# One subtraction of an attention kernel issued on GpSimd instead of VectorE

## The chip, the cores and the metric

The kernel runs on all 8 cores of one Trainium2 chip, the same program on each, with no traffic between cores. Core c takes batch c // 2 and one half of its 4096 positions as queries (2048 of them, "own"), with all 4096 positions as keys. The time is device time of the slowest core in microseconds.

## What is computed

X is (4, 4096, 1024), 16 heads of width 64, EPS = 1e-4:

```
xn = layernorm(x)
Q, K, V, G = split(xn @ W_in + b_in)              # per head, 64 columns each
W = (EPS + sqrt(max(|q|^2 + |k|^2 - 2 q.k, 0))) ** -2
A = (W / (EPS + sum_s W)) @ V
x = x + concat_heads(G * A) @ W_out + b_out
x = x + layernorm(x) @ sign(weight).T
```

The kernel doesn't take the square root. With D the squared distance, (EPS + sqrt(D))^-2 is about 1/D - 2 EPS D^-1.5, and both powers come from one logarithm: L = Ln(D), Ea = Exp(-L), Ebc = Exp(-1.5 L + ln(2 EPS)), W = Ea - Ebc. The last of these, `wb`, is the subtraction that the change touches.

## The kernel before

The program is written as five queues, one for each engine, with semaphores between them. `st(engine, fn, waits, inc)` appends one instruction to an engine's queue; each engine takes its queue strictly in order and stops at the first wait that is not met. So the order in which the Python code calls `st` is the order of each queue.

Before attention, the input is normalised and transposed into XnT, and head 0 is projected. After attention come the output projection, the second layernorm and the product with the signs. None of this touches the changed line. In between, attention runs over 16 heads, 4 query blocks of 512 to a head, and 16 rounds r to a block, each for 256 keys. Two rounds make a step s of 4 x 512 = 2048 score columns; there are 32 steps to a head, 8 to a query block. What a step does:

- `emit_S` (L480, TensorE): scores of a round, two matmuls into pS. Kaug and Qaug have 66 rows, with the squared norms as two of them, so pS is the squared distance. pS has two buffers, one to a round.
- `emit_c1` (L489, ScalarE): Lb = Ln(pS), once a round.
- `emit_c24` (L495, L498, ScalarE): Ea and Ebc from Lb, once a step. Ea has two buffers and waits for the subtraction two steps back; Ebc has one, and waits for the subtraction one step back.
- `emit_c3` (L503, VectorE before): wb = Ea - Ebc, 128x2048, out in bf16, two buffers. It waits for Ebc and for the matmuls that read the wb of two steps back.
- `emit_A` (L517, TensorE): four matmuls for a step, Vs by wb, summed over the block's 8 steps in pA (row 64 sums W, since column 64 of Vs is 1).

At the end of a query block `emit_epilogue_a` copies pA to A_sb on VectorE (L531), moves its row 64 to partition 0 by a DMA issued on GpSimd (L537), takes Ln and Exp of it on ScalarE (L541, L543) and splits the result in two bf16 rows (L546, L548). `emit_epilogue_b` spreads them over partitions by matmul, multiplies, and for odd heads moves Htmp into H by another GpSimd DMA (L593).

The projections of the next head are spliced into the rounds of this one. `stage_proj` writes them down in 61 groups, the first one empty: 4 for Q, 8 for K, 32 for V, 4 for G, then 8 for the k norms and 4 for the q norms. `splice` appends about one group per round. The weights' loads on SyncE and their casts to bf16 on VectorE (L318) go in as one piece in round 0 of a head (`flush_w`). A Q, K, V or G group is eight matmuls (L333, L364) into pp and one copy out on VectorE. A norm group is a square on VectorE (KQsq, L390), one matmul (L398), a copy to the single buffer k2row on VectorE (L402) and a DMA issued on GpSimd (L407, L412) that puts it in row 64 or 65 of the next head's Qaug or Kaug. The copy waits until the DMA before it has landed. The scores of a new head wait, by a nop on GpSimd (L418), for all of these DMAs.

The main loop for round r, shortened:

```python
        emit_c1(r)
        if r % 2 == 1:
            emit_c24(r // 2)
            emit_c3(r // 2)
        if r + 1 < NTOT and not nxt_head_start:
            emit_S(r + 1)
        if r % 2 == 0 and r >= 2:
...
            emit_A(2 * s - 2)
            emit_A(2 * s - 1)
...
        splice(slot_in_head + 1, NQC * NREG)
```

Of the kernel before, what the change touches and what calls it, by code (L numbers as in the profile page):

```python
# [34 lines left out]
def build_nc():  # L35
# [11 lines left out]
    def st(engine, fn, waits=(), inc=None, inc_n=1):  # L47
        if inc is not None:
            inc.n += inc_n
        cur_steps[0][engine].append((list(waits), fn, inc, inc_n))  # L50
# [449 lines left out]
           waits=[(s_c3, s)], inc=s_c2)  # L500

    def emit_c3(s):
        st("vector", lambda e, s=s: e.tensor_tensor(  # L503
            out=wb[s % 2][:], in0=Ea[s % 2][:], in1=Ebc[:], op=ALU.subtract),
           waits=[(s_c2, 2 * s + 2), (s_wcons, max(0, 4 * s - 4))], inc=s_c3)

# [94 lines left out]
    for r in range(NTOT):  # L601
# [7 lines left out]
# [3 lines that stand above are left out]
# [3 lines left out]
        if r % 2 == 0 and r >= 2:  # L615
# [3 lines left out]
            s = r // 2  # L619
# [302 lines left out]
```

How the kernel before makes its waits and increments, by code:

```python
            def run(eng):  # L861
                for waits, fn, inc, inc_n in steps[name]:
                    for (sm, val) in waits:
                        if val > 0:
                            eng.wait_ge(sm.h, val)
                    inst = fn(eng)
                    if inc is not None:
                        inst.then_inc(inc.h, inc_n)
```

## Time and profile before

| | |
|---|---|
| median of 3 runs | 4886.65 us (4886.46 to 4899.19) |
| the profiled execution | 4886.19 us, span of its slowest core 4884.6 us |
| spans of the 8 cores | 4874.3 to 4884.6 us |
| mean granted TensorE clock | 0.668 to 0.676 of full |
| from the first Ebc to the last (attention) | 345.9 to 4533.5 us of the span |

The profile is of one execution, on the slowest core (core 5). Engines are named PE (TensorE matmul), PEld (its weight loads), DVE (VectorE), ACT (ScalarE), POOL (GpSimd) and SP (SyncE); L503 is line 503 of the kernel. In a timeline a row gives the start, the length, the engine, the line and the operation; in brackets stands how long the engine had been idle before it and what ended that. A row of POOL's DMA is the issue, not the transfer.

### The profile page before, as it was taken

How to read it: one execution, taken by the hardware profiler on the slowest of the kernel's cores; microseconds unless marked ns; L12 is line 12 of the kernel's file. 1: busy time of each engine (PE TensorE's matmuls, PEld its weight loads, DVE VectorE, ACT ScalarE, POOL GpSimd, SP SyncE). 2: the span in 40 equal slices, each digit the busy share in tenths (PEclk: the TensorE clock that was granted, in tenths of full speed). 3: DMA queues.
4: the chain of work that ended last, by engine and by line, in shares of the span. 5: the costliest groups of instructions: out<-in, count | busy, mean ns of one | idle time of the engine just before them, and what ended most of it. 6: DMA issues, size and time to landing. Idle time of an engine off the chain costs nothing.

```text
span 4884.6 us, 45463 instructions; the slowest of 8 cores (4874.3 to 4884.6 us)
## 1 busy us (share of the span) xinstructions
PE 2654.0 (54%) x11472; PEld 1049.1 (21%) x11472; DVE 2167.3 (44%) x2630; ACT 3027.2 (62%) x2321; POOL 146.3 (3%) x300
## 2 busy tenths in 40 slices
PE   1156465665655554656555565556465555645535
PEld 1122122222212121212222121212122222211202
DVE  4534444444444444444444444444444444443344
ACT  2218676676768585867767585858676776768100
POOL 0000000000000000000000000000000000000000
PEclk9977575667666675767576666666576766655757
DMA  2200000000000000000000000000000000000312
GB/s 75 66 18 1 5 6 2 10 1 10 2 10 1 9 2 10 1 1 10 2 10 1 9 2 10 1 9 2 6 5 1 10 2 8 1 1 2 104 35 69
DMA packets 41383, 64.14 MB, mean 13 GB/s; under 512 B 12992, under 2 KB 29376, under 8 KB 40128
## 3 DMA queue, kind: packets, MB, share of 16 engines
q1 hardware_dynamic: 31680, 58.79, 3.8%
q0 software_dynamic: 9472, 2.45, 0.3%
q8 instruction: 123, 2.02, 0.2%
q14 instruction: 108, 0.88, 0.1%
HBM read 50.39 MB, written 8.39 MB: 12 GB/s over the span
## 4 chain that ended last, share of the span: by engine, by line
PE 27%; ACT 25%; issue 23%; DVE 18%; DMA 6%; DVEq 1%; ACTq 0%; SPq 0%; POOLq 0%
ACT Ebc L498 13%; DVE wb L503 10%; ACT Lb L489 8%; PE pA L517 7%; PE pS L480 7%; PE pp L333 7%; DMA Wst<-w_in 2%; DMA rsrow<-A_sb 2%; PE pp L364 1%; ACT Ea L495 1%; PE pp L398 1%; PE pS L836 1%; PE pS L682 1%; DVE KQsq L390 1%; DVE A_sb L531 1%
## 5 line engine op out<-in xcount | busy, mean ns | idle before, releaser
L503 DVE TENSOR_TENSOR wb<-Ea,Ebc 128x2048 bf16<-128x2048 f32 x512 | 1173.4, 2292 | 782.0 <-ACT Ebc L498 775.0
L489 ACT ACTIVATE Lb<-pS 128x1024 f32<-128x1024 f32 x1024 | 1019.7, 1015 | 752.3 <-PE pS L480 749.0
L517 PE MATMUL pA<-wb,Vs 128*65 128x512 bf16 x2048 | 826.3, 547 | 1036.8 <-DVE wb L503 1036.7
L498 ACT ACTIVATE Ebc<-Lb 128x2048 bf16<-128x2048 f32 x512 | 970.4, 1895 | 113.7 <-DVE wb L503 113.7
L495 ACT ACTIVATE Ea<-Lb 128x2048 f32<-128x2048 f32 x512 | 978.8, 1912 | 77.2 <-ACT Lb L489 3.4
L480 PE MATMUL pS<-Qaug,Kaug 66*128 66x512 bf16 x2048 | 877.5, 530 | 199.3 <-ACT Lb L489 142.9
L517 PEld LDWEIGHTS pA<-wb,Vs 128*65 128x65 bf16 x2048 | 293.3, 144 | 1536.1 <-issue 1506.5
L333 PE MATMUL pp<-XnT,Wbf 128*64 128x512 bf16 x2048 | 551.3, 419 | 24.6 <-DVE Wbf L318 24.6
L364 PEld LDWEIGHTS pp<-Wbf,XnT 128*128 128x128 bf16 x4096 | 278.3, 125 | 233.2 <-issue 223.5
L333 PEld LDWEIGHTS pp<-XnT,Wbf 128*64 128x64 bf16 x2048 | 223.8, 119 | 345.9 <-issue 207.3
L371 DVE CAST Vs<-pp 128x64 bf16<-128x64 f32 x512 | 113.4, 222 | 405.3 <-PE pp L364 403.7
L364 PE MATMUL pp<-Wbf,XnT 128*128 128x64 bf16 x4096 | 289.3, 229 | 3.7 <-DVE Vs L371 3.7
L541 ACT ACTIVATE rlrow<-rsrow 1x512 f32<-1x512 f32 x64 | 40.3, 630 | 402.5 <-DMA rsrow<-A_sb 402.5
L480 PEld LDWEIGHTS pS<-Qaug,Kaug 66*128 66x128 bf16 x2048 | 173.4, 116 | 462.5 <-issue 458.7
L402 DVE CAST k2row<-pp 1x512 bf16<-1x512 f32 x192 | 130.3, 679 | 262.9 <-PE pp L398 230.3
L398 PE MATMUL pp<-KQsq,ones_col 64*1 64x512 bf16 x128 | 71.1, 555 | 322.5 <-DVE KQsq L390 322.5
L352 DVE TENSOR_SCALAR Kaug<-pp,bin_sb 64x512 bf16<-64x512 f32 x128 | 95.5, 746 | 156.1 <-PE pp L333 154.2
L224 PE MATMUL pT<-c_identb,xnf 128*128 128x128 bf16 x256 | 32.4, 307 | 200.4 <-DVE xnf L212 200.4
L546 DVE CAST rnhl<-rsrow 1x512 bf16<-1x512 f32 x64 | 26.5, 415 | 248.3 <-ACT rsrow L543 248.3
L531 DVE TENSOR_SCALAR A_sb<-pA,ebv 65x512 f32<-65x512 f32 x64 | 47.8, 747 | 194.8 <-PE pA L517 194.8
L398 PE MATMUL pp<-KQsq,q_col 64*1 64x512 bf16 x64 | 37.2, 582 | 169.9 <-DVE KQsq L390 169.9
L537 POOL DMA_DIRECT2D rsrow<-A_sb x64 | 31.4, 491 | 2753.0 <-DVE A_sb L531 2707.2
(85 smaller groups left out, 1210.2 us busy)
## 6 DMA issues: line engine op xcount, KB each, us to landing
xst<-x SPq DMA_DIRECT2D x32, 512.0 KB, 3.8
Wst<-w_in SPq DMA_DIRECT2D x128, 128.0 KB, 2.1
XT<-xT SPq DMA_DIRECT2D x8, 1024.0 KB, 17.5
y<-XT SPq DMA_DIRECT2D x32, 256.0 KB, 2.4
wst<-w_out SPq DMA_DIRECT2D x8, 512.0 KB, 4.7
wst<-w_ffn SPq DMA_DIRECT2D x8, 512.0 KB, 3.9
Kaug<-k2row POOLq DMA_DIRECT2D x128, 1.0 KB, 1.5
H<-Htmp POOLq DMA_DIRECT2D x32, 64.0 KB, 1.9
```

What stands on the lines that cost most here:

```text
L333: return e.matmul(ppt[0:64, :], Wbf[hb][:, c * 256 + cols0:c * 256 + cols0 + 64], XnT[:, c * SLEN + n * 512:c * SLEN + (n + 1) * 512], sta ...
L364: return e.matmul(ppt[0:128, 0:64], XnT[:, c * SLEN + t * 128:c * SLEN + (t + 1) * 128], Wbf[hb][:, c * 256 + 128:c * 256 + 192], start=(c ...
L371: return e.tensor_copy(out=Vs[hb][:, t * 65:t * 65 + 64], in_=ppt[0:128, 0:64])
L398: return e.matmul(ppt[0:1, :], scol[0:64, :], KQsq[sl][:], start=True, stop=True)
L402: return e.tensor_copy(out=k2row[:], in_=ppt[0:1, :])
L480: st("tensor", lambda e, hb=hb, qc=qc, stile=stile, ps=ps, k=k: e.matmul(pS[ps][:, k * 512:(k + 1) * 512], Kaug[hb][:, stile * 128:(stile ...
L489: st("scalar", lambda e, ps=ps, sb=(r // 2) % 2, half=r % 2: e.activation(out=Lb[sb][:, half * 1024:half * 1024 + 1024], in_=pS[ps][:], fu ...
L495: st("scalar", lambda e, s=s: e.activation(out=Ea[s % 2][:], in_=Lb[s % 2][:], func=AF.Exp, scale=-1.0), waits=[(s_c1, 2 * s + 2), (s_c3, ...
L498: st("scalar", lambda e, s=s: e.activation(out=Ebc[:], in_=Lb[s % 2][:], func=AF.Exp, scale=-1.5, bias=LN2EPS), waits=[(s_c3, s)], inc=s_c2)
L503: st("vector", lambda e, s=s: e.tensor_tensor(out=wb[s % 2][:], in0=Ea[s % 2][:], in1=Ebc[:], op=ALU.subtract), waits=[(s_c2, 2 * s + 2), ...
L517: st("tensor", lambda e, hb=hb, stile=stile, ws=s % 2, half=r % 2, k=k, bk=bk: e.matmul(pAb[bk][0:65, :], Vs[hb][:, stile * 65:stile * 65 ...
L531: st("vector", lambda e, asl=asl, bk=bk, h=h: e.tensor_scalar(out=A_sb[asl][:], in0=pAb[bk][0:65, :], scalar1=ebv[0:65, h:h + 1], scalar2= ...
```

## The change

The subtraction is issued on GpSimd. Its operands, its waits and its signal are the same, and so is its place in the order of the code; it is now one of GpSimd's queue, together with the DMA issues named above, instead of VectorE's. No buffer changes.

```diff
     def emit_c3(s):
-        st("vector", lambda e, s=s: e.tensor_tensor(
+        st("gpsimd", lambda e, s=s: e.tensor_tensor(
             out=wb[s % 2][:], in0=Ea[s % 2][:], in1=Ebc[:], op=ALU.subtract),
            waits=[(s_c2, 2 * s + 2), (s_wcons, max(0, 4 * s - 4))], inc=s_c3)
```

## Rows read from the trace of the kernel before

**Rows 1.** The page: busy time by engine, and the chain that ended last.

```profile
PE 2654.0 (54%) x11472; PEld 1049.1 (21%) x11472; DVE 2167.3 (44%) x2630; ACT 3027.2 (62%) x2321; POOL 146.3 (3%) x300
...
PE 27%; ACT 25%; issue 23%; DVE 18%; DMA 6%; DVEq 1%; ACTq 0%; SPq 0%; POOLq 0%
```

**Rows 2.** The page, costliest groups: busy us, mean ns, idle before and its releaser.

```profile
L503 DVE TENSOR_TENSOR wb<-Ea,Ebc 128x2048 bf16<-128x2048 f32 x512 | 1173.4, 2292 | 782.0 <-ACT Ebc L498 775.0
...
L498 ACT ACTIVATE Ebc<-Lb 128x2048 bf16<-128x2048 f32 x512 | 970.4, 1895 | 113.7 <-DVE wb L503 113.7
```

**Rows 3.** Stages from Ebc to Ebc, head 6, and head 15: us, busy by engine, clock.

```profile
1933.58:1957.77 24.19, 11.74 (x40) 4.20 (x39) 9.59 (x14) 11.40 (x9) 0.54 (x1) 0.65 0.15 46
1957.77:1990.73 32.96, 27.83 (x129) 11.15 (x129) 19.06 (x16) 28.39 (x22) 0.00 (x0) 1.00 0.00 0
...
2005.48:2046.94 41.46, 24.29 (x141) 11.81 (x141) 19.55 (x21) 39.36 (x30) 0.00 (x0) 0.66 0.00 0
...
2114.96:2130.91 15.95, 10.18 (x31) 3.52 (x31) 9.34 (x9) 11.31 (x10) 0.00 (x0) 0.79 0.00 0
2130.91:2179.80 48.89, 22.71 (x48) 5.56 (x48) 21.97 (x25) 28.23 (x21) 4.87 (x10) 0.51 0.00 1
2179.80:2199.88 20.08, 5.40 (x12) 1.59 (x13) 5.25 (x7) 6.90 (x7) 1.46 (x3) 0.50 0.00 1
4333.18:4533.54 200.36, 112.88 (x254) 37.11 (x252) 81.89 (x48) 175.61 (x132) 3.08 (x6) 0.51 0.02 5
```

**Rows 4.** Timeline, a V stage of head 6: start us, length us.

```profile
2064.60 1.89 PE L517 MATMUL pA<-wb,Vs 128*65 128x512 bf16 x4 [4.43 <-DVE wb L503]
...
2072.14 1.90 ACT L498 ACTIVATE Ebc<-Lb 128x2048 bf16<-128x2048 f32 x1
...
2074.20 2.29 DVE L503 TENSOR_TENSOR wb<-Ea,Ebc 128x2048 bf16<-128x2048 f32 x1 [1.37 <-ACT Ebc L498]
...
2076.64 1.68 PE L517 MATMUL pA<-wb,Vs 128*65 128x512 bf16 x4 [2.52 <-DVE wb L503]
```

**Rows 5.** Timeline, the K stage of head 6.

```profile
1975.66 1.02 PE L517 MATMUL pA<-wb,Vs 128*65 128x512 bf16 x4 [1.40 <-DVE wb L503]
...
1984.53 1.90 ACT L498 ACTIVATE Ebc<-Lb 128x2048 bf16<-128x2048 f32 x1
...
1989.04 1.02 PE L517 MATMUL pA<-wb,Vs 128*65 128x512 bf16 x4 [1.40 <-DVE wb L503]
```

**Rows 6.** Timeline, the end of a query block.

```profile
2052.71 0.75 DVE L531 TENSOR_SCALAR A_sb<-pA,ebv 65x512 f32<-65x512 f32 x1 [1.28 <-PE pA L517]
...
2054.13 0.49 POOL L537 DMA_DIRECT2D rsrow<-A_sb  x1 [54.57 <-DVE A_sb L531]
2055.77 0.63 ACT L541 ACTIVATE rlrow<-rsrow 1x512 f32<-1x512 f32 x1 [6.03 <-DMA rsrow<-A_sb]
```

**Rows 7.** Timeline, the norm groups of head 6, and its last DMA and A.

```profile
2144.75 0.41 DVE L390 TENSOR_TENSOR KQsq<-Kaug 64x512 bf16<-64x512 bf16 x1
...
2146.75 1.91 PE L517 MATMUL pA<-wb,Vs 128*65 128x512 bf16 x4
...
2149.36 0.68 DVE L402 CAST k2row<-pp 1x512 bf16<-1x512 f32 x1 [1.82 <-PE pp L398]
...
2150.80 0.49 POOL L407 DMA_DIRECT2D Kaug<-k2row  x1 [2.70 <-DVEq L302]
...
2186.88 0.49 POOL L412 DMA_DIRECT2D Qaug<-k2row  x1 [5.90 <-DVEq L302]
...
2190.45 1.91 PE L517 MATMUL pA<-wb,Vs 128*65 128x512 bf16 x4
```

**Rows 8.** Timeline, the start of head 6: last weight cast, wb, first Q group.

```profile
1944.20 0.29 DVE L318 CAST Wbf<-Wst 128x256 bf16<-128x256 f32 x1 [0.27 <-DMA Wst<-w_in]
...
1944.83 2.29 DVE L503 TENSOR_TENSOR wb<-Ea,Ebc 128x2048 bf16<-128x2048 f32 x1 [0.34 <-DVE Wbf L318]
...
1949.19 2.58 PE L333 MATMUL pp<-XnT,Wbf 128*64 128x512 bf16 x8
```

## The prediction

> **What bounds the kernel now.** I read four views in turn: the page, one head cut into stages, short stretches of the timeline inside each stage, and the chain of waits beside them. The page says that no engine is full: TensorE has matmuls 54% of the time, ScalarE is busy 62%, VectorE 44%, GpSimd (POOL) 3% [rows 1]. The chain that ended last changes hands all the time, with 18% of it VectorE work and 23% time in which nothing the profile shows was awaited [rows 1]. So this is a ring of handovers, and what counts is which ring closes last in each stage.
>
> One step is 2048 score columns: two Ln of half that width and the Exps Ea and Ebc of 1.9 us each on ScalarE, then the subtraction wb = Ea - Ebc of 2.292 us on VectorE [rows 2], then four matmuls with V. There are 32 steps to a head and 16 heads, 512 in all. I date a step by the start of its Ebc, and call the subtraction C and the four matmuls A. The stages of head 6 [rows 3], in order: steps 0-1 (weights of the next head and its first Q groups) 24.19 us; 2-6 (Q and K groups, full clock) 32.96; 8-14 (V groups, granted clock 0.66) 41.46; 24-25 (G groups) 15.95; 26-30 (norm rows k2 and q2) 48.89; 31 (change of head) 20.08. Steps 7, 15 and 23, each the end of a query block, and 16-22, a second V stage, repeat what is shown and are left out. Head 15, with nothing spliced in, has 28 steps of 5.68 us and its block ends in 200.36 us.
>
> **Why a V step takes what it takes.** A of one step starts at 2064.60; the Ebc two steps later starts 7.54 us after it, C 2.06 after that, the next A 2.44 after C's start [rows 4]. TensorE runs its queue in order: the scores of step s+2 stand behind A(s), so C -> A -> scores -> Ln -> Ea -> Ebc -> C is a ring over two steps, 12.04 us or 6.02 a step. ScalarE's own work, 5.68 a step, lies just under it. In the K stage the same ring is 8.87 from A to Ebc and 4.51 from there to the next A, 13.38 us for two steps, and TensorE idles 1.40 us in front of A, released by C [rows 5].
>
> **The change.** It moves 512 C from VectorE to POOL with the same waits and the same signal. VectorE loses 512 x 2.292 us, and its queue no longer holds anything behind C. POOL gets C ahead of the DMA issues emitted after it (k2row, rsrow, H) and behind those emitted before it.
>
> **Length of C on POOL.** The trace of before has no POOL arithmetic on a tile that could price it. From below: POOL as quick as VectorE, 2.29 us. From above: both inputs fetched one after the other, 2 x 2.29 = 4.58, and a slower handover besides: POOL's DMA issue starts 0.67 us after VectorE's A_sb is done [rows 6], where A follows C's end by 0.15 [rows 4], so 5.1. In between lies 3.8, two passes at ScalarE's 1.9 [rows 2]. I take 4.58 with VectorE's handover, d = 2.29 longer than now: nearer to the upper end, because POOL's only rows are slow starters (0.5 us for an issue [rows 6]) and nothing shows two inputs in one pass there.
>
> VectorE's 2292 ns is also what the Trainium skill (GPSIMD Engine Reference, section Performance versus the Vector engine) gives for a 2048-column fp32 tensor_tensor, and the trace agrees; the page puts GpSimd at 4497 ns, which no run here shows yet. By it the total below would be 27 us less, and the page's advice speaks against this change.
>
> **Stage by stage, change per head.**
> V stages. The ring becomes 12.04 + 2.29 = 14.33, 7.17 a step. Ebc has one buffer, so Ebc(s+1) waits for C(s): at least 2.07 + 4.58 + 0.1 = 6.75 a step, just under. Started from rest, the seven steps come at 6.8, then rings: odd ones end at 6.8 + 3 x 14.33 = 49.8 us, against 41.46. +8.3, twice.
> K stage. First ring: A starts 6.8 after Ebc(2), and then 8.87 more, but TensorE has idled some 4 us and starts low: A takes 1.89 instead of 1.02 [rows 4, 5] and the group behind it 2.58 instead of 1.91 [rows 8], +1.5; 17.2 us. Second ring 13.38 + 2.29 = 15.7, last step about 7.8: 40.7 against 32.96. +7.7 (5.4 with no clock lost, 9.6 with the loss in both rings and the last step).
> Block ends (steps 7, 15, 23). ScalarE stands with its Ln of the row sums behind C -> A -> A_sb -> POOL's DMA -> Ln; the DMA needs A_sb anyway, so POOL's queue adds nothing. +2.3 each, 6.9.
> Steps 24-25: one ring, +2.3.
> Steps 26-30. Now 9.57 a step (one was 10.61), because KQsq stands in VectorE's queue behind C, the k2 matmul in TensorE's queue waits for KQsq, and the second scores stand behind that: KQsq starts 2144.75, as C ends, then come A 2146.75, k2row 2149.36 and its DMA issue 2150.80 [rows 7]. After the change KQsq is free, but C(s+1) stands in POOL's queue behind a k2row DMA that itself hangs on A(s). From the end T of C(s): A at 0.15; k2row 2.61 later, 2.75; DMA issue 1.44 later, 4.2, and 0.5 long; C(s+1) at 4.7. A step is 4.7 + 4.58 = 9.3. ScalarE's path lies beside it: behind A come a k2 matmul, the scores, a second k2 matmul and scores, so the step's second Ln at about T + 6, Ea at 7.1 and Ebc at 8.9, before C(s+1) ends at 9.3. The landing, 1.6 us after an issue [rows 6], is covered. Entering the stage Ebc(27) only waits for C(26), 6.7. So 6.7 + 4 x 9.3 = 43.9 against 5 x 9.57 = 47.9. -4.0: the VectorE queue's stall goes to POOL's queue.
> Step 31. Scores of the new head wait for the head's last k2row DMA, and A(31) stands behind them: issue 2186.88, A 2190.45, 3.57 later [rows 7]. That DMA will stand behind C(31). Counted from T of step 30, Ebc(31) starts at 0.1 and A(31) at 4.7 + 4.58 + 3.6 = 12.9, 12.8 apart; now it is 2179.80 [rows 3] to 2190.45, 10.65. +2.2.
> Steps 0-1. C(0) stands behind eight casts of weights that wait for loads, the last at 1944.20; it starts at 1944.83, and after A the first Q group at 1949.19 [rows 8]. Moved to POOL, C(0) and A are over before the casts, and the Q group can start at the last cast's end, 1944.5: -4.7. But POOL would be reading SBUF beside the casts, for which the trace has no row; if each pair of casts were held back until C ends, nothing is left. I take half, -2.3.
> Sum: 16.6 + 7.7 + 6.9 + 2.3 - 4.0 + 2.2 - 2.3 = 29.4 us a head, for 15 heads 441. Head 15: 28 x (6.75 - 5.68) + 4 x 2.3 = 39. Together +480. The profiled execution took 4886.2 us (span 4884.6), the median is 4886.65; so **5366 us**.
>
> Each microsecond of C counts half per step in the rings (19 steps, 9.5), once in the 4 block ends, once in 24-25 and five times in 26-30: 19.5 a head, 32 in head 15, 324 in all. With 5.1 us: 5535. With 4.0: 5178.
>
> **Rivals.**
> (a) Faster: POOL runs C nearly as quickly as VectorE. Then the rings are as before, steps 26-30 fall to about 7 us, the head change is even, the head start gains: 29.4 - 19.5 x 2.29 = -15.3 us a head for 15 heads, head 15 as now: 4657 us. The sign turns where C is 480 / 324 = 1.5 us shorter than I take it, at 3.1. For it speaks that VectorE reads two inputs in one pass, 2.29 us, and ScalarE one in 1.9 [rows 2]; against it, that POOL's rows are slow ones.
> (b) Covered: C stays under ScalarE's work, no change, 4887. ScalarE leaves 5.68 - 2.29 = 3.4 us of apparent room. Against it: the ring of 12.04 and the single Ebc buffer (a C above 5.68 - 2.17 = 3.5 lengthens even head 15). It needs a C of 3.05 to 3.15, where loss in the rings and gain in 26-30 balance.
> (c) Mutual blocking: VectorE and POOL hold each other up in SBUF. The casts at the head start wait for C(0) and C(1), the 2.3 a head is lost: 5366 + 35 = 5400; if C also waits for VectorE's KQsq and casts (0.41 and 0.29 us [rows 7, 8]), up to 12 x 0.41 a head more, 5475. The Trainium skill (SBUF — State Buffer, section Who interferes with whom) states such a lock for casts and for two-input VectorE operations against GpSimd reads; no row of before can bear it out, since nothing reads on POOL.
> (d) C much longer than two passes, with the write a third one, 6.87 us: 5366 + 2.29 x 324 = 6108.
> (e) The clock: with longer idle TensorE stays at 1.2 GHz through the K stage; rings there are then +1.9 a head dearer, 5395. Inside the forecast's range.
>
> **Chances.** Forecast (C between 3.9 and 5.2, with e) 0.63, (c) 0.20, (a) 0.04, (b) 0.03, (d) 0.08, other 0.02 (slower). Under 0.3% (15 us) this kernel's runs can't be told from no change. Slower 0.93, same 0.02, faster 0.05. The range 5150 to 5590 takes in a C from 3.9 to 5.2 us and (c).
>
> **What would show it.** POOL TENSOR_TENSOR x512 at 4.4 to 5.1 us. In V stages 7.1 to 7.2 a step, Ebc waiting for C; in 26-30 9.3 a step, with C on POOL starting right at a k2row DMA issue's end; KQsq no longer waiting for C; block ends 2.3 longer; the Q group of a new head within 5 us of the last cast or not; casts still 0.29 or stretched. Wrong would be made by C's length first (324 us for each us), then by a handover to POOL longer than 0.15.

## The result

The changed kernel took 5279.97 us (median of 8 runs, 5276.55 to 5292.11) against 4894.88 for the kernel before in the same series: a ratio of 1.0786, 95% interval 1.0766 to 1.0805. The forecast was 5366 us with a range of 5150 to 5590. The profiled execution took 5278.8 us, 392.6 more than the one of before; the working below is made against that difference. Fast executions are compared throughout.

The page of the changed kernel, where it answers to [rows 1] and [rows 2]; the columns are the same:

```profile
PE 2779.8 (53%) x11472; PEld 1078.8 (20%) x11472; DVE 1286.6 (24%) x2118; ACT 3064.7 (58%) x2321; POOL 2225.7 (42%) x812
...
PE 30%; POOL 25%; ACT 17%; issue 13%; DVE 9%; DMA 5%; DVEq 0%; POOLq 0%; ACTq 0%; SPq 0%
...
L503 POOL TENSOR_TENSOR wb<-Ea,Ebc 128x2048 bf16<-128x2048 f32 x512 | 2080.5, 4063 | 1711.5 <-ACT Ebc L498 1337.2
...
L390 DVE TENSOR_TENSOR KQsq<-Kaug 64x512 bf16<-64x512 bf16 x128 | 161.5, 1262 | 31.5 <-DVE k2row L402 31.0
L318 DVE CAST Wbf<-Wst 128x256 bf16<-128x256 f32 x128 | 134.3, 1049 | 116.0 <-DMA Wst<-w_in 97.6
```

The subtraction (C) takes 4.063 us on POOL, 1.77 times as long as on VectorE, and a quarter of the chain is now POOL's. VectorE is busy for 24% of the span instead of 44%, and the kernel is slower all the same. Two VectorE operations that nobody touched have grown: the casts of the weights from 294 to 1049 ns in the mean, the squares KQsq from 414 to 1262.

The same stages of head 6 as in [rows 3], and head 15, in the changed kernel:

```profile
2081.08:2109.45 28.37, 12.77 (x42) 4.51 (x40) 13.14 (x13) 11.40 (x9) 8.67 (x3) 0.61 0.14 40
2109.45:2149.34 39.89, 28.66 (x107) 10.82 (x106) 7.19 (x10) 28.44 (x21) 20.32 (x5) 0.89 0.00 0
2165.38:2213.26 47.88, 25.11 (x137) 11.65 (x136) 3.91 (x13) 40.18 (x30) 28.43 (x7) 0.61 0.00 0
2291.26:2308.11 16.85, 9.12 (x31) 3.32 (x31) 4.40 (x7) 11.40 (x9) 8.19 (x3) 0.80 0.00 0
2308.11:2349.75 41.64, 20.71 (x44) 4.49 (x45) 20.96 (x18) 28.68 (x21) 24.96 (x15) 0.54 0.00 1
2349.75:2371.03 21.28, 7.66 (x17) 2.13 (x17) 3.73 (x7) 6.89 (x7) 5.67 (x5) 0.50 0.00 0
4695.44:4924.89 229.45, 112.97 (x251) 37.16 (x250) 11.11 (x17) 179.34 (x132) 129.02 (x37) 0.51 0.01 4
```

One head is one sample, so the next table takes the starts of all Ebc from both timelines and averages each stage over heads 1 to 14. The last column is the working on record with one number replaced, a C of 4.06 in place of 4.58; the head start was forecast without C's length, so it stays.

| steps | before | after | difference | forecast, C = 4.58 | forecast, C = 4.06 |
|---|---|---|---|---|---|
| 0-1, head start | 24.89 | 28.13 | +3.2 | -2.3 | -2.3 |
| 2-6, Q and K groups | 33.22 | 40.85 | +7.6 | +7.7 | +6.4 |
| 7, 15, 23, block ends | 41.61 | 46.68 | +5.1 | +6.9 | +5.3 |
| 8-14 and 16-22, V groups | 82.89 | 95.29 | +12.4 | +16.6 | +13.0 |
| 24-25 | 15.77 | 16.92 | +1.2 | +2.3 | +1.8 |
| 26-30, norm groups | 48.00 | 41.47 | -6.5 | -4.0 | -6.6 |
| 31, change of head | 20.17 | 21.36 | +1.2 | +2.2 | +1.7 |
| one head | 266.5 | 290.7 | +24.2 | +29.4 | +19.3 |

15 x 24.15 is 362 us, and head 15 adds 29 (200.4 to 229.5): 391 of the 392.6. Every stage but the first agrees with the last column to 1.2 us. The first has the wrong sign.

The ring of a V stage in the changed kernel, in the timeline, beside [rows 4]:

```profile
2235.26 1.91 ACT L498 ACTIVATE Ebc<-Lb 128x2048 bf16<-128x2048 f32 x1 [0.48 <-POOL wb L503]
2235.41 1.89 PE L517 MATMUL pA<-wb,Vs 128*65 128x512 bf16 x4 [6.24 <-POOL wb L503]
...
2237.37 4.06 POOL L503 TENSOR_TENSOR wb<-Ea,Ebc 128x2048 bf16<-128x2048 f32 x1 [2.21 <-PE pA L517]
...
2242.83 1.89 ACT L498 ACTIVATE Ebc<-Lb 128x2048 bf16<-128x2048 f32 x1
...
2244.93 4.06 POOL L503 TENSOR_TENSOR wb<-Ea,Ebc 128x2048 bf16<-128x2048 f32 x1 [3.50 <-ACT Ebc L498]
```

Both limits that the forecast named are there, in turn. The first Ebc waits for C, released by POOL, and a step so bound takes 6.26 us; the next is bound by the ring through TensorE and takes 7.60 (means over steps 8 to 14). The pair is 13.86 us; 12.04 plus 1.77 is 13.81. The releaser named at 2237.37 is a matmul of pA, but C waits only for the matmuls of two steps back, which are long done; what it waited for is Ebc, which ended 0.20 us before, at 2237.17.

The norm stage, where the forecast put C behind a k2row DMA issue in POOL's queue:

```profile
2318.95 4.07 POOL L503 TENSOR_TENSOR wb<-Ea,Ebc 128x2048 bf16<-128x2048 f32 x1
...
2323.16 1.89 PE L517 MATMUL pA<-wb,Vs 128*65 128x512 bf16 x4 [3.01 <-POOL wb L503]
...
2325.73 0.68 DVE L402 CAST k2row<-pp 1x512 bf16<-1x512 f32 x1 [2.43 <-PE pp L398]
...
2327.19 0.48 POOL L407 DMA_DIRECT2D Kaug<-k2row  x1 [3.71 <-DVEq L302]
...
2327.69 4.08 POOL L503 TENSOR_TENSOR wb<-Ea,Ebc 128x2048 bf16<-128x2048 f32 x1
...
2329.73 2.32 DVE L390 TENSOR_TENSOR KQsq<-Kaug 64x512 bf16<-64x512 bf16 x1 [0.27 <-DVE k2row L402]
...
2331.91 1.89 PE L517 MATMUL pA<-wb,Vs 128*65 128x512 bf16 x4 [3.01 <-POOL wb L503]
```

C starts at 2327.69, 0.02 us after the issue ends; its Ebc had ended at 2325.13, 2.6 us before. From the end of the C before it, 2323.02, A comes after 0.14 us, k2row after 2.71, the issue after 4.17 and C after 4.67; the forecast had 0.15, 2.75, 4.2 and 4.7. The step is 8.73 to 8.9 us; 4.7 + 4.06 is 8.76. KQsq starts in the middle of C and ends with it, at 2332.05 to C's 2331.77.

And the head start, beside [rows 8]. Here is the surprise:

```profile
2083.55 4.42 DVE L318 CAST Wbf<-Wst 128x256 bf16<-128x256 f32 x1 [0.27 <-DVE Wbf L318]
2083.73 4.08 POOL L503 TENSOR_TENSOR wb<-Ea,Ebc 128x2048 bf16<-128x2048 f32 x1
...
2090.02 4.06 POOL L503 TENSOR_TENSOR wb<-Ea,Ebc 128x2048 bf16<-128x2048 f32 x1 [2.21 <-PE pA L517]
2090.37 3.85 DVE L318 CAST Wbf<-Wst 128x256 bf16<-128x256 f32 x1 [1.83 <-DMA Wst<-w_in]
...
2099.55 0.29 DVE L318 CAST Wbf<-Wst 128x256 bf16<-128x256 f32 x1 [1.41 <-DMA Wst<-w_in]
2100.21 3.25 PE L333 MATMUL pp<-XnT,Wbf 128*64 128x512 bf16 x8 [10.25 <-DVE Wbf L318]
```

A cast of 0.29 us takes 4.42 beside C and ends 0.16 after it; another takes 3.85 and ends 0.14 after its C. The loads come two at a time and wait for the casts, so the delays pass on to the loads: the last cast ends 18.8 us after Ebc(0) began, against 10.9 before. Over heads 1 to 14 the eight casts together take 6.9 us more (2.35 to 9.26) and the last ends 6.8 us later (11.15 to 17.92): nothing of the hold is absorbed. C(0) no longer waits for the casts, and that doesn't help the first Q group, which waits for the last of them: it starts 18.27 us after Ebc(0) in place of 15.87.

### The profile page after: what moved, and what is told of

The parts are those of the page before. It is cut to its first block, busy times and chain, and to the rows that moved or that the text cites. A ratio compares the mean times of both kernels' runs of the same rounds, so it can differ in the third digit from the quotient of the medians.

```text
span 5277.2 us, 45463 instructions; the slowest of 8 cores (5261.5 to 5277.2 us)
## 1 busy us (share of the span) xinstructions
PE 2779.8 (53%) x11472; PEld 1078.8 (20%) x11472; DVE 1286.6 (24%) x2118; ACT 3064.7 (58%) x2321; POOL 2225.7 (42%) x812
## 4 chain that ended last, share of the span: by engine, by line
PE 30%; POOL 25%; ACT 17%; issue 13%; DVE 9%; DMA 5%; DVEq 0%; POOLq 0%; ACTq 0%; SPq 0%
POOL wb L503 25%; PE pA L517 10%; ACT Ebc L498 9%; PE pp L333 8%; PE pS L480 6%; ACT Lb L489 4%; DVE Wbf L318 2%; DMA Wst<-w_in 2%; ACT Ea L495 2%; DMA rsrow<-A_sb 2%; PE pp L364 1%; DVE k2row L402 1%; PE pS L836 1%; PE pS L682 1%; PE pp L398 1%
## 5 line engine op out<-in xcount | busy, mean ns | idle before, releaser
L503 POOL TENSOR_TENSOR wb<-Ea,Ebc 128x2048 bf16<-128x2048 f32 x512 | 2080.5, 4063 | 1711.5 <-ACT Ebc L498 1337.2
L517 PE MATMUL pA<-wb,Vs 128*65 128x512 bf16 x2048 | 851.3, 561 | 1506.9 <-POOL wb L503 1506.9
L480 PE MATMUL pS<-Qaug,Kaug 66*128 66x512 bf16 x2048 | 915.9, 551 | 228.2 <-ACT Lb L489 140.1
L333 PE MATMUL pp<-XnT,Wbf 128*64 128x512 bf16 x2048 | 597.7, 446 | 160.5 <-DVE Wbf L318 160.5
L364 PEld LDWEIGHTS pp<-Wbf,XnT 128*128 128x128 bf16 x4096 | 294.7, 130 | 249.7 <-issue 242.4
L333 PEld LDWEIGHTS pp<-XnT,Wbf 128*64 128x64 bf16 x2048 | 235.7, 125 | 512.5 <-issue 391.9
L364 PE MATMUL pp<-Wbf,XnT 128*128 128x64 bf16 x4096 | 305.5, 236 | 3.7 <-DVE Vs L371 3.7
L407 POOL DMA_DIRECT2D Kaug<-k2row x128 | 64.9, 507 | 306.7 <-DVEq L302 305.3
L390 DVE TENSOR_TENSOR KQsq<-Kaug 64x512 bf16<-64x512 bf16 x128 | 161.5, 1262 | 31.5 <-DVE k2row L402 31.0
L318 DVE CAST Wbf<-Wst 128x256 bf16<-128x256 f32 x128 | 134.3, 1049 | 116.0 <-DMA Wst<-w_in 97.6
```

The source lines that it names most:

```text
L318: st("vector", lambda e, c=c, sl=sl, hb=hb: e.tensor_copy(out=Wbf[hb][:, c * 256:(c + 1) * 256], in_=Wst[sl][:]), waits=[(s_wld[sl], s_wld ...
L333: return e.matmul(ppt[0:64, :], Wbf[hb][:, c * 256 + cols0:c * 256 + cols0 + 64], XnT[:, c * SLEN + n * 512:c * SLEN + (n + 1) * 512], sta ...
L364: return e.matmul(ppt[0:128, 0:64], XnT[:, c * SLEN + t * 128:c * SLEN + (t + 1) * 128], Wbf[hb][:, c * 256 + 128:c * 256 + 192], start=(c ...
L390: st("vector", lambda e, srcb=srcb, n=n, sl=sl: e.tensor_tensor(out=KQsq[sl][:], in0=srcb[0:64, n * 512:(n + 1) * 512], in1=srcb[0:64, n * ...
L480: st("tensor", lambda e, hb=hb, qc=qc, stile=stile, ps=ps, k=k: e.matmul(pS[ps][:, k * 512:(k + 1) * 512], Kaug[hb][:, stile * 128:(stile ...
L503: st("gpsimd", lambda e, s=s: e.tensor_tensor(out=wb[s % 2][:], in0=Ea[s % 2][:], in1=Ebc[:], op=ALU.subtract), waits=[(s_c2, 2 * s + 2), ...
```

## The experiments

Times are medians; each ratio is to the kernel before in the same job (4890.08 us in the first four, 4887.48 in the last four). Stage times are means over heads 1 to 14, as above.

**POOL in the norm groups alone.**

```diff
-        st("vector", lambda e, s=s: e.tensor_tensor(
+        st("gpsimd" if 25 <= s % 32 <= 30 else "vector", lambda e, s=s: e.tensor_tensor(
```

> The subtraction is on POOL in steps 25 to 30 of each head alone (norm groups), on VectorE in the others. Theory (VectorE's queue holds the k2/q2 square behind the subtraction, and that is what a norm step of 9.57 us pays): steps 26 to 30 take 8.8 us as in the changed kernel, all other stages as before, so 15 x 6.5 us less than before: 4790 us. Rival (the norm steps gain only because the rings ahead of them were stretched, TensorE arriving with work done): no gain here, 4885 or more.

Measured: 4825.25 us, ratio 0.9866 (0.9851 to 0.9881). Steps 26 to 30 take 41.48 us, to 0.01 what they take in the changed kernel and 6.5 less than before, while steps 2 to 25 are as before (within 0.1 us but for the block ends, 41.2 against 41.6). So the gain is the norm stage's own and not borrowed from stretched rings ahead of it; the rival falls. The forecast was 35 us too low, 26 of them for two things it left out: step 31 takes 1.4 us more (21.52), since its last DMA is issued 8.8 us after Ebc(31) instead of 7.1 (head 6), and head 15 has no norm groups and loses 6 us in those steps.

**VectorE in steps 0 and 1 alone.**

```diff
-        st("gpsimd", lambda e, s=s: e.tensor_tensor(
+        st("gpsimd" if s % 32 >= 2 else "vector", lambda e, s=s: e.tensor_tensor(
```

> The subtraction is on POOL except in steps 0 and 1 of each head. Theory (casts at the head start are held while POOL subtracts): casts back to 0.29 us each, steps 0 and 1 back to about 24.9 us from 28.1, and a little off step 2; 15 x 3.5 us less than the changed kernel, 5228 us. Rival (the loads or the clock make the long head start, not the neighbour in SBUF): casts stay long or the head start stays at 28, 5280 us.

Measured: 5223.45 us, ratio 1.0687 (1.0667 to 1.0707). The casts' group in this kernel, listed by form:

```profile
L318 DVE CAST Wbf<-Wst 128x256 bf16<-128x256 f32 x128 | 37.6, 294 | 117.7 <-DMA Wst<-w_in 106.0 <-DVEq L597 5.8 <-DVE Wbf L318 5.3
```

All 128 casts are back to 294 ns and steps 0 and 1 to 25.26 us from 28.13, 2.9 us less, and 3.8 over the whole head. The loads are the same as in the changed kernel; the neighbour of the casts is gone. Since C(0) then stands behind the casts again, this is the price of the hold less what C's early start was worth.

**The square first, all on VectorE.** In norm groups the first VectorE step (KQsq) is appended ahead of the subtraction.

```diff
             emit_c24(r // 2)
+            square_first(r % (NQC * NREG) + 1, NQC * NREG)
             emit_c3(r // 2)
...
+    def square_first(frac_num, frac_den):
+        if staging_groups is None:
+            return
+        target = len(staging_groups) * frac_num // frac_den
+        for g in staging_groups[moved_groups[0]:target]:
+            if g.get("norm"):
+                steps["vector"].append(g["vector"].pop(0))
```

> Everything on VectorE as before, but in norm groups the square (KQsq) of an odd round is put ahead of the subtraction in VectorE's queue. Theory (the stall is one of queue order alone): the k2 matmul and the second scores no longer wait for the subtraction; the next limit is the one k2row buffer, k2row after its DMA has landed: about 6.6 us a step in place of 9.57 in steps 25 to 31, 15 x 6 x 3 us less, 4620 us. Rival (the norm step is bound by the chain k2row, DMA, landing, k2row, two a step): 8.5 us or more a step, 4790 us or more.

Measured: 4669.35 us, ratio 0.9549 (0.9533 to 0.9565). Steps 26 to 30 take 34.00 us in place of 48.00 (5.7, 7.9, then 6.6 and 7.2 in turn) and step 31 18.82. The stall of 9.57 us was one of queue order, and it could be removed without moving any work. The expectation, 4620, was 49 us too low: it took 3 us off each of six steps, where the norm steps and step 31 gave 15.4 a head together and the other stages took 0.7 of it back. Moving C to POOL cured the same stall for less than half of that, because C then stood behind the DMA issue instead. In this kernel's norm stage k2row waits for the landing of its own last DMA:

```profile
2055.53 0.48 POOL L409 DMA_DIRECT2D Kaug<-k2row  x1 [3.00 <-DVEq L302]
...
2057.09 0.68 DVE L404 CAST k2row<-pp 1x512 bf16<-1x512 f32 x1 [1.64 <-DMA Kaug<-k2row]
...
2058.92 2.29 DVE L513 TENSOR_TENSOR wb<-Ea,Ebc 128x2048 bf16<-128x2048 f32 x1 [0.47 <-ACT Ebc L508]
```

**POOL over half of the columns.** Columns 1024 to 2047 of wb are left out and keep ones.

```diff
-            out=wb[s % 2][:], in0=Ea[s % 2][:], in1=Ebc[:], op=ALU.subtract),
+            out=wb[s % 2][:, 0:1024], in0=Ea[s % 2][:, 0:1024], in1=Ebc[:, 0:1024],
+            op=ALU.subtract),
```

> The subtraction is on POOL everywhere but over 1024 of its 2048 columns; the other half is left out (wb's second half keeps ones from a memset at the start). Theory (length of the subtraction decides, POOL's queue and handover cost next to nothing): it takes about 2.05 us, rings fall to ScalarE's 5.7 us a step, norm steps to 6.8, casts are held at most 2 us: faster than before, 4575 us. Rival (being on POOL costs by handover and by the DMA issues in its queue, whatever the length): not faster than before, 4885 us or more.

Measured: 4610.24 us, ratio 0.9426 (0.9412 to 0.944). C takes 2.12 us on POOL here, VectorE's length within 0.17, and the kernel beats the one before by 280 us though C is on POOL everywhere. So with a C as short as VectorE's, being on POOL leaves no loss, and the rival falls. Its casts are still held, 558 ns in the mean, and norm steps take 6.8 to 7.5 us after a first of 5.7: 33.87 us for steps 26 to 30, as with the square first (34.00). So the gain over the kernel before is in the main that of queue order. This is near to the forecast's rival (a): 4657 was worked out for a C of 2.29.

**Casts on ScalarE, the subtraction on VectorE, and the same with the subtraction on POOL.** The loads and VectorE's part of the weights stay in round 0; the casts follow Ebc of step 0 in ScalarE's queue (round 1), and a load waits for the cast itself.

```diff
...
-            st("vector", lambda e, c=c, sl=sl, hb=hb: e.tensor_copy(
-                out=Wbf[hb][:, c * 256:(c + 1) * 256], in_=Wst[sl][:]),
-               waits=[(s_wld[sl], s_wld[sl].n)], inc=s_wcast)
+            st("scalar", lambda e, c=c, sl=sl, hb=hb: e.activation(
+                out=Wbf[hb][:, c * 256:(c + 1) * 256], in_=Wst[sl][:], func=AF.Copy),
+               waits=[(s_wld[sl], s_wld[sl].n), (s_hbf[hb], h // 2)], inc=s_wcast)
...
```

> The subtraction on VectorE as before; the weight casts go to ScalarE, behind Ebc of step 0. Theory: the subtraction of step 0 no longer stands behind the casts, ScalarE gives up some 9 us to waiting for loads that it would have idled anyway; steps 0 and 1 come to 20.5 us from 24.9: 15 x 4.4 less, 4825 us. Rival (ScalarE's wait delays its own next Ln more than it frees): 4890 or more.

Measured: 4843.05 us, ratio 0.9912 (0.9897 to 0.9927). Steps 0 and 1 take 21.91 us in place of 24.89, 1.4 less than hoped for; 2.7 of the 3.0 remain over the head (263.9 us). Head 0, whose own weights go the same way, adds to it: the first Ebc comes 13 us earlier and head 0 takes 7 us longer, so some 6 of the 44 us are not of the head starts of heads 1 to 14.

> The subtraction on POOL everywhere, the weight casts on ScalarE, behind Ebc of step 0. If VectorE and POOL hold each other up in SBUF and ScalarE is outside of that, the casts are not stretched though POOL subtracts beside them (about 0.4 us each), and steps 0 and 1 come to 21 us from 28.1: 15 x 7 less than the changed kernel, 5175 us. Rival (any engine's pass over SBUF is stretched beside POOL's): casts of several us on ScalarE too, no gain over 5223.

Measured: 5222.28 us, ratio 1.0687 (1.0671 to 1.0703). The casts and C in step 0 of head 6:

```profile
2054.07 4.07 POOL L508 TENSOR_TENSOR wb<-Ea,Ebc 128x2048 bf16<-128x2048 f32 x1
2056.25 0.96 ACT L318 ACTIVATE Wbf<-Wst 128x256 bf16<-128x256 f32 x2 [2.33 <-DMA Wst<-w_in]
```

Two casts in 0.96 us while POOL subtracts, 412 ns each in the mean here and 412 in the kernel with C on VectorE: ScalarE isn't held. The time by itself is the rival's 5223 and would not have told the two apart; the casts do, and the rival falls. Steps 0 and 1 came to 21.54 us as forecast, 6.6 less than in the changed kernel, but steps 2 to 6 took 44.42, 3.6 more: C(1) now starts at 2068.78, after ScalarE's casts, and A(1), at 2072.99, holds TensorE up, where in the changed kernel C(1) was over long before. Of the 6.6 us, 3.7 are left at the end of the head (286.98). The gain was real and half of it was given back one stage later.

**Half on each engine.** Columns 0 to 1023 on VectorE, the others on POOL, with a semaphore for each half.

```diff
+        for eng, a, b, sem in (("vector", 0, 1024, s_c3), ("gpsimd", 1024, 2048, s_c3p)):
+            st(eng, lambda e, s=s, a=a, b=b: e.tensor_tensor(
+                out=wb[s % 2][:, a:b], in0=Ea[s % 2][:, a:b], in1=Ebc[:, a:b],
+                op=ALU.subtract),
+               waits=[(s_c2, 2 * s + 2), (s_wcons, max(0, 4 * s - 4))], inc=sem)
```

> The subtraction in two halves at once: columns 0 to 1023 on VectorE, 1024 to 2047 on POOL, both released by Ebc. If the two run beside each other, 1.2 and 2.1 us, the step is as with one of 2.1: the rings as before or 0.1 shorter, norm steps about 9.5, 4870 us. If they exclude each other (theory, from the casts and KQsq that end with POOL's subtraction), one of the halves shows 3.3 us instead of its own length, rings longer by some 1.0 per two steps, 5010 us.

Measured: 5055.59 us, ratio 1.0342 (1.0325 to 1.0359). Two steps of the timeline:

```profile
2050.25 2.12 POOL L505 TENSOR_TENSOR wb<-Ea,Ebc 128x1024 bf16<-128x1024 f32 x1 [3.02 <-ACT Ebc L499]
...
2050.70 2.76 DVE L505 TENSOR_TENSOR wb<-Ea,Ebc 128x1024 bf16<-128x1024 f32 x1
...
2057.94 1.23 DVE L505 TENSOR_TENSOR wb<-Ea,Ebc 128x1024 bf16<-128x1024 f32 x1 [0.61 <-ACT Ebc L499]
...
2057.97 3.17 POOL L505 TENSOR_TENSOR wb<-Ea,Ebc 128x1024 bf16<-128x1024 f32 x1 [5.59 <-ACT Ebc L499]
```

The halves take 1.23 us on VectorE and 2.12 on POOL when nothing stands in the way. Where POOL is first, VectorE's takes 2.76 and ends 1.1 us after POOL's; where VectorE is first, by 0.03 us, POOL's takes 3.17. VectorE is first in 428 of the 512; there POOL's half has a median of 3.17, and the pair is nearly as long as the sum of the two alone, 3.35. The means over all 512 are 1.32 and 3.00. The theory's size was right (5010 against 5056), its place only in part: the V stages lost 0.8 and 1.1 us each, and the norm steps most, 10.48 us for 9.57, since KQsq, behind VectorE's half, runs beside POOL's half and is held as well (1.32 us in the mean).

**Both good edits, all on VectorE.** The square first, and the casts on ScalarE.

> Everything on VectorE, square first in norm groups, and the weight casts on ScalarE behind Ebc of step 0. Both edits touch different stages, so their gains add: 4669 less 15 x 4.4, 4603 us; faster than both kernels. Rival: the head start's gain is taken back by the stage behind it: 4669.

Measured: 4613.63 us, ratio 0.9439 (0.9425 to 0.9453). Steps 0 and 1 21.68, 26 to 30 34.07: each stage as in the run with that edit alone. This is the version that beats both kernels with the whole computation, by 274 us and 666 us.

## Why the prediction was right, and where it was not

**The rings.** Right. V stages: 13.86 us a pair against 13.81 from the ring plus C's growth, and between them steps bound by the single Ebc buffer. C's length is what the time hangs on: in the runs with the whole C or half of it on POOL everywhere, 4.06 us gives 5280 and 2.12 gives 4610, 345 us for each us; the working had 324 for the whole range.

**C's length.** The mis-sized term: 4.58 was taken and 4.063 measured, 324 x 0.52 = 168 us too much. Two one-after-the-other passes at VectorE's rate was the wrong model for it; two at ScalarE's 1.9 [rows 2], 3.8, lay nearer. The run over 1024 columns gives 2.12, so about 1.94 us for a further 1024, 1.9 ns a column. The Trainium skill's figure (GPSIMD Engine Reference, section Performance versus the Vector engine) is 4497 ns for fp32; the measured 4063 ns, with one bf16 input and a bf16 output, is 10% less and decides.

**POOL's handover.** Taken as VectorE's; right. C starts 0.20 us after Ebc's end in the median against 0.17 on VectorE, and A follows C's end by 0.15 to 0.25 us in both kernels. The 0.67 us to a DMA issue was no guide to it.

**Head start.** Wrong in sign: -2.3 forecast, +3.2 measured. The step that failed is the one where I took half of a gain of 4.7 between "no hold" and "nothing left", for want of a row with POOL reading SBUF. Nothing left was not the worst: the casts are held until C ends and the loads stand behind the casts, so the first Q group comes later than before. That is rival (c), to which I gave 0.20; its mechanism was right, and its price too low: it took 35 us off the gain and ended at no change in these steps, where 3.2 x 15 = 49 us more were lost. The runs that bear on it: casts back to 294 ns with C on VectorE beside them, casts on ScalarE undisturbed, and the split, in which POOL waits for VectorE. The Trainium skill (SBUF — State Buffer, section Who interferes with whom) says that whichever of VectorE and GpSimd issues first keeps the ports that they share for its whole instruction, and names casts and two-input VectorE operations among those that contend; the traces agree on both kinds (a cast took up to 4.42 us, a square up to 4.04) and, in the split, on both orders. One row doesn't seem to fit: the cast at 2083.55 starts 0.18 us before C and is held all the same. POOL was issuing a DMA just then (2083.18 to 2083.72). Six heads begin in this way; in a seventh (2663.84), with the same issue and the same 0.18 us, the cast takes its 0.29. What decides it stays open.

**Norm groups.** Right in mechanism and size: -6.5 a head against -6.6 with the measured C. The change does cure a stall, and puts a smaller one in its place. The other part of rival (c), C waiting for VectorE's short operations, is real but next to nothing: in three heads a cast begins 0.01 us before C(0), takes its 0.29, and C takes 4.20 to 4.21 us in place of 4.06. No other C is longer than 4.1 us; KQsq comes after C, not before:

```profile
1793.03 0.29 DVE L318 CAST Wbf<-Wst 128x256 bf16<-128x256 f32 x1 [0.27 <-DVE Wbf L318]
1793.04 4.21 POOL L503 TENSOR_TENSOR wb<-Ea,Ebc 128x2048 bf16<-128x2048 f32 x1 [7.72 <-ACT Ebc L498]
```

**K stage.** +7.6 against 6.4: I gave the clock loss to one ring of two. Pairs take 17.3 us (11.03 and 6.25 in turn) against 13.38 + 1.77 = 15.15. The stage's last step, taken at 7.8, came at 6.25 and hides part of that. Behind a wait of 3.76 us for C, A still ran at the high rate and the group behind it at the low one:

```profile
2132.57 1.02 PE L517 MATMUL pA<-wb,Vs 128*65 128x512 bf16 x4 [3.76 <-POOL wb L503]
2133.53 3.50 PE L333 MATMUL pp<-XnT,Wbf 128*64 128x512 bf16 x8
```

In the kernel before the same group, behind a wait of 1.40 us for C [rows 5], took 1.91:

```profile
1976.61 1.91 PE L333 MATMUL pp<-XnT,Wbf 128*64 128x512 bf16 x8
```

That is 1.6 us more, once in each pair, and the stage's granted clock is 0.89 after 1.00 [rows 3]. (The prediction takes its 1.91 from [rows 8], which don't show it; this row does.) No run tested the clock by itself, so this part is read from the trace and not shown by an experiment.

**The sum.** -168 (C's length), +83 (head start) and +18 (clock) take 480 to 413. The other stages of heads 0 to 14 came out some 27 us lower together, and head 15 7 us higher than its 22, which gives the measured 393. The forecast was nearer than its terms deserved, by luck: the largest two errors had opposite signs.

## What to carry to other kernels

Before moving an operation to an idle engine, follow the ring it sits in: what counts is its length there, not the busy share of either engine, and here each microsecond of it is worth about 345 (5280 us with 4.06, 4610 with 2.12). Look at what stood behind it in the old queue, for that is the gain, and try to have that gain by order alone: one square put ahead of the subtraction gave 220 us, nearly all of it in the norm steps; moving the subtraction gave 98 there and cost 490 elsewhere. Check which untouched operations of VectorE run beside the new POOL operation, and what loads wait for them.

## What the runs showed that was not expected

A held cast is a small line on the page, 0.76 us more in the mean over 128 casts, but two of the eight in a head bear it all, and the two-buffer loads took the whole delay on: the last cast ends 6.8 us later. KQsq tripled, from 414 to 1262 ns, without harm where it was looked at: the square at 2329.73 ends at 2332.05, while A, which stands ahead of its matmul, runs to 2333.80. And in the split kernel two engines on one subtraction were slower than VectorE alone, 5056 against 4887.
